# A fused decoder layer on one core: a new timetable by slots, six slots of attention output, and sums of v taken from wider products

## The reference

```python
scores = einsum('bsnh,btnh->bnst', k, q) / sqrt(32)
scores = triu(scores) + -10000.0 * tril(ones, k=-1)
attn = softmax(scores, axis=2)
out = einsum('bnkq,bknh->bqnh', attn, v)          # then @ Wo + bo
x = layernorm(x + attention(x))
x = layernorm(x + wkv(w, u, k=x, v=ctx))          # a scan over t, 512 channels
h = silu(x @ Wg.T) * (x @ Wu.T)                   # Wg, Wu, Wd: (int - 128) * scale
x = layernorm(x + h @ Wd.T)
```

## Time and profile before

| | us |
|---|---|
| median of 3 runs | 807.76 (806.75 to 809.14) |
| profiled execution | 813.54 |
| its span | 811.7 |
| PE busy in the span | 738.0 (91%) |
| DVE, ACT, POOL busy | 514.1, 437.6, 271.4 |
| mean granted clock of PE | 0.966 |

### The profile page before, as it was taken

The page is one execution under the profiler, slowest core; times in us unless marked ns, Lnnn a source line. Parts: engine busy times, 40 slices in busy tenths (PEclk is TensorE's granted clock), DMA queues, the critical chain, the costliest instruction groups (busy, mean ns, idle before and its releaser), DMA issues.

```text
span 811.7 us, 11923 instructions
## 1 busy us (share of the span) xinstructions
PE 738.0 (91%) x4256; PEld 402.2 (50%) x4256; DVE 514.1 (63%) x1132; ACT 437.6 (54%) x1035; POOL 271.4 (33%) x285
## 2 busy tenths in 40 slices
PE   6899799988989969979788999999998999999996
PEld 2465456654566536645454544445443444444443
DVE  3565575887998867678865377985758462342124
ACT  5678776877667767656587456405452234113310
POOL 2001310326571154233211454445655233113310
PEclk9899899997999979989999999999999999999999
DMA  8435384341324233253200810000000000010001
GB/s 265 118 91 169 96 205 130 92 117 43 89 78 139 91 83 92 74 131 57 78 1 1 156 52 0 14 27 14 0 1 20 34 0 1 14 40 0 1 14 39
DMA packets 45387, 54.17 MB, mean 67 GB/s; under 512 B 4752, under 2 KB 34704, under 8 KB 45328
## 3 DMA queue, kind: packets, MB, share of 16 engines
q1 hardware_dynamic: 42064, 47.11, 19.4%
q0 software_dynamic: 3264, 6.29, 4.5%
HBM read 47.10 MB, written 12.58 MB: 74 GB/s over the span
## 4 chain that ended last, share of the span: by engine, by line
PE 52%; DVE 17%; ACT 9%; POOL 8%; issue 8%; DMA 4%; SPq 1%; POOLq 0%; DVEq 0%; ACTq 0%
PE psb L779 16%; PE psb L665 5%; PE psb L714 5%; PE psb L792 4%; PE psb L790 4%; DVE ek L1114 4%; PE psb L759 4%; PE psb L681 3%; PE psb L727 3%; PE psb L703 2%; POOL ct L1267 2%; POOL ek L1271 2%; ACT ee L872 2%; DVE x L1089 2%; DVE ee L1018 2%
## 5 line engine op out<-in xcount | busy, mean ns | idle before, releaser
L1018 DVE CUSTOM_DVE_ANT_0 ee<-psb,mask,clip 128x512 f32<-128x512 f32 (+3 forms) x256 | 131.9, 534 | 62.9 <-PE psb L703 62.4
L872 ACT ACTIVATE ee<-ee,nm 128x512 f32<-128x512 f32 (+3 forms) x256 | 142.6, 558 | 33.8 <-DVE nm L1018 33.5
L1301 POOL TENSOR_TENSOR hl<-hf,hh 128x512 f16<-128x512 f32 x64 | 78.0, 1218 | 162.1 <-ACT hh L949 162.1
L883 ACT ACTIVATE ee<-psb 128x512 f32<-128x512 f32 (+1 forms) x192 | 100.0, 521 | 55.9 <-PE psb L714 37.5
L714 PE MATMUL psb<-ident,ee 128*128 128x128 f32 x640 | 108.8, 287 | 23.4 <-ACT ee L883 23.3
L949 ACT ACTIVATE hh<-hf 128x512 bf16<-128x512 f32 x64 | 40.3, 629 | 136.0 <-DVE hf L1141 131.2
L1141 DVE SCALAR_TENSOR_TENSOR hf<-th,c,psb 128x512 f32<-128x512 f32 x60 | 44.2, 737 | 105.2 <-PE psb L779 75.4
L714 PEld LDWEIGHTS psb<-ident,ee 128*128 128x128 f32 x640 | 77.2, 147 | 50.9 <-ACT ee L883 33.3
L792 PE MATMUL psb<-wd,hl 128*128 128x512 f16 x256 | 97.7, 382 | 3.7 <-POOL hl L1301 3.7
L790 PE MATMUL psb<-wd,hh 128*128 128x512 f16 x256 | 97.5, 381 | 0.9 <-ACT hh L949 0.9
L779 PE MATMUL psb<-x2h,wg 128*128 128x512 f16 x256 | 97.0, 379 | 1.3 <-ACT x2h L927 1.3
(11 more groups left out here) (111 smaller groups left out, 1205.9 us busy)
## 6 DMA issues: line engine op xcount, KB each, us to landing
qs<-parts SPq DMA_DIRECT2D x64, 128.0 KB, 2.9
ks<-parts SPq DMA_DIRECT2D x64, 128.0 KB, 3.2
parts<-qhl SPq DMA_DIRECT2D x16, 256.0 KB, 2.2
parts<-khl SPq DMA_DIRECT2D x16, 256.0 KB, 2.3
x<-in_x SPq DMA_DIRECT2D x4, 1024.0 KB, 7.4
ct<-in_ctxT SPq DMA_DIRECT2D x4, 1024.0 KB, 6.8
out<-x SPq DMA_DIRECT2D x16, 256.0 KB, 2.0
xt<-in_xT SPq DMA_DIRECT2D x14, 256.0 KB, 3.9
```

Source lines behind the costliest of these rows:

```text
L872: e.activation(dst, dst, ACT.Exp, bias=NM[:, n % 4, col:col + 1], scale=-1.0, accum_out=DEN[:, n % 4, col:col + 1]).then_inc(sem("exp"), 1)
L883: e.activation(ET[h][:, base:base + width], PSB[:, bank["turn", H, item], 0:width], ACT.Copy).then_inc(sem("et"), 1)
L1018: e.tensor_tensor_reduce(E[H % 3][:, EOFF[i]:EOFF[i] + w], PSB[:, bank["score", H, i], 0:w], MASK[:, S - w:S], -SC, CLIP[:, i:i + 1], ALU. ...
L1301: e.tensor_tensor(HS[it][1][:], ring(b, it)[1][:], HS[it][0][:], ALU.subtract).then_inc(sem("hl"), 1)
```

## The change

1. `timetable()` takes the slot of each piece from tables by group or batch, in place of a few offsets for all: `QK_AT`, `V_AT`, `WO_AT` (where the parts of a product are spread), `FIN_AT` (for each group the slots, counted from the start of the next, of `pv`, of `sv` with the first `spread`, and of the second), `XLOAD` and `XSPLIT`, `WKV_AT`, `YT_AT`, `X2_AT`, the loads and the subtraction of the zero point. `WAIT` sets how many slots behind its product each further step stands. `stack` becomes a piece of its own with a slot.
2. `oh` and `ol` have six slots in place of four (`OHS`); group n waits for `wo` of the batch of group n - 6. `HOLD` goes.
3. `later` and its copy go. The triangle of `sv` now takes in the diagonal, so that the first column of each block is the block's sum; `t1` reads its operand shifted by one column, and two additions of one column each (`SUF`) make the sums over later blocks, once a group. The last position's weight is set to zero by a product with `some` on POOL.
4. `EX` and `RX` become one tile `WIDE`; the second widening (`widen`) waits until PE has transposed the first.
5. `x2h` and `x2l` stand one and two slots behind `x2t`. The zero point of `wd` is taken off at 16 slots, not two a slot.

```diff
-WKV_AT = {(0, 0): (6, 6), (0, 1): (6, 15), (0, 2): (7, 4), (0, 3): (7, 10), (1, 0): (10, 6), (1, 1): (11, 4),
-QOFF, V0, V1, U0, U1, U2, W0, W1, W2, W3 = 11, 2, 11, 3, 4, 13, 3, 12, 0, 6
-XLOAD, XSPLIT = (14, 15, 18, 19), (1, 2, 5, 6)
-NSLOT, SP2, HOLD = (3, 1, 1, 1), 3, 11
+OHS = 6
+QK_AT = {2: (6, 19), 3: (22, 31), 4: (36, 46), 5: (62, 67), 6: (71, 79), 7: (88, 94), 8: (109, 112), 9: (123, 128),
+FIN_AT = {0: (2, 1, 11), 1: (2, 2, 13), 2: (2, 1, 11), 3: (1, 4, 9), 4: (2, 0, 10), 5: (2, 2, 11), 6: (0, 0, 9),
+XLOAD = {1: (11, 22, 28, 31), 2: (73, 86, 90, 95), 3: (156, 160, 162, 164)}
+XSPLIT = {1: (33, 33, 35, 36), 2: (96, 98, 100, 107), 3: (162, 168, 171, 173)}
+WKV_AT = {(0, 0): 109, (0, 1): 118, (0, 2): 124, (0, 3): 134, (1, 0): 176, (1, 1): 186, (1, 2): 212, (1, 3): 226}
...
-        def later(b):
-            bk = bank["later", b]
...
-            for g in range(T):
-                for j in range(1, T):
-                    mm = e.matmul(PSB[:, bk, 4 * g:4 * g + 4], VV[:, b % 2, j, g * P:(g + 1) * P],
-                                  LT[:, P + 4 * j:P + 4 * j + 4], start=(j == 1), stop=(j == T - 1))
...
             act.wait_ge(*by("t3", n))
-            if b:
-                act.wait_ge(*by("wo", b - 1, T - 1))
-            e.activation(oh[:, g, :], EB[:], ACT.Identity, bias=BV[:, g:g + 1]).then_inc(sem("oh"), 1)
+            if n >= OHS:
+                act.wait_ge(*by("wo", (n - OHS) // T, T - 1))
+            e.activation(oh[:, n % OHS, :], EB[:], ACT.Identity, bias=BV[:, g:g + 1]).then_inc(sem("oh"), 1)
...
+            sums = PSB[:, bank["sv", n], :]
+            e.tensor_scalar(SUF[:, 1:2], sums[:, 2 * P:2 * P + 1], sums[:, 3 * P:3 * P + 1], None, ALU.add).then_inc(sem("suf"), 1)
             dve.wait_ge(*by("eb", n))
-            dve.wait_ge(*by("suf", b))
-            for i in range(T):
...
+            e.tensor_tensor(EB[:, 3 * P - 1:S - 1], sums[:, 3 * P:S], EB[:, 3 * P - 1:S - 1], ALU.mult)
+            dve.wait_ge(sem("suf"), 2 * n + 1)
+            e.tensor_tensor(SUF[:, 0:1], sums[:, P:P + 1], SUF[:, 1:2], ALU.add).then_inc(sem("suf"), 1)
+            for i, rest in ((2, sums[:, 3 * P:3 * P + 1]), (1, SUF[:, 1:2]), (0, SUF[:, 0:1])):
...
+            e.tensor_tensor(EM[:, n % 4, :], EM[:, n % 4, :], SOME[:], ALU.mult).then_inc(sem("some"), 1)
...
+        def widen(n):
+            pool.wait_ge(*by("expand", n))
+            pool.wait_ge(sem("spread0"), n + 1)
```

More of the change, by code:

```diff
@@ L256, in yt @@
         add("yt", b, t)
-        late(3, residual)
+        late(WAIT["r2"], residual)
     def x2t(b, c):
@@ new lines, in spread_over, with piece, split_wo @@
+    def spread_over(units, first, end):
+        for k, u in enumerate(units):
+            at(first + k * (end - first) // len(units), u)
+    def piece(slot, *what):
+        at(slot, lambda: add(*what))
+    def split_wo():
+        add("split_wo")
+        add("load_ct", 0)
+    spread_over(vs0[3:], 0, 9)
+    for n, span in QK_AT.items():
+        spread_over(qk_units(n), *span)
+        begun = 16 * (n - 2) + 12
+        at(max(begun, span[1] + WAIT["low"]), lambda n=n: (tt.flush(("put", n, "k")), add("stack", n)))
@@ L368, in timetable @@
+    for which, slot in WKV_AT.items():
+        at(slot, lambda which=which: wkv(*which))
     slot_turn = ((1, 2), None, (0, 0), (0, 1))
```

275 lines of the change are left out of this document (121 added, 154 removed).

## The result

The changed kernel takes 765.74 us (median of 4 runs, 762.17 to 766.27) against 808.45 us of the kernel before (4 runs in the same series). The ratio is 0.946, interval 0.9422 to 0.9499; on the 807.76 us of the time shown ahead that is 764.1, a gain of 44. One caution: in a second series, of five rounds, it gave 769.07 us (6 runs) and a ratio of 0.9524, interval 0.9499 to 0.9549, a gain of 38. So the gain is 38 to 44 us. The forecast was 31, with a range from 765 to 799: the first series lies just outside it, the second inside. The direction was right, the size about a quarter too small.

A forecast was written before the change was run, and what follows sets the result against it. PE's work plus its waits and half clock, mostly in attention, was taken as the bound. Terms -12.0 + 1 - 19 - 5 + 2 + 1 + 3.5 - 3 = -31.5 took 813.5 to 782, stated as 777 against the 807.8 median; range 765 to 799.

The forecast's parts named there:

- The narrow products: Four blocks of `later` on PE's path: 10.3 us go, plus 1.7 of half clock; 12.0 taken, bounds 7 to 12.
- The triangle: Product `sv` on PE: the triangle keeps its 128 columns, so it costs PE nothing more.
- The splits: Three stalls where PE waits for ACT and ACT for late loads of x: gain 19 of 25.8 us, bounds 10 to 25.
- The projection: At 345 to 365 us PE idles, mostly for `ol` of the last group: gain 5 of 7.9 us.
- DVE's stretch in slots 112 to 143: From 200 to 240 us DVE sets the pace; group 7 loses work to group 8: 3 back, 4 charged, net +1.
- the 15 below which the prediction called itself wrong: Sign of failure: PE's busy time in attention falls by less than 15 us.
- the first stall: Batch 1's split of x: ACT still waits about 2.7 us, PE meets it directly; 4.7 of 7.4 us left.
- It goes better: Rival, 763 us: all 25.8 of stalls and 12 of products go, DVE's stretches lose half their idle time; chance 0.07.
- The rival of the clock: Slots 48 to 95 get thinner PE work and half clock there uses up the gain; 812 us; chance 0.06, slower.
- In slots 216 to 223 ... +3.5: Four `x2l` on DVE atop norm and reciprocals, with nine parts of `qk` and `wo` on PE: 3.5 us more.
- In the feed-forward ... -3: PE idles 2.0 and 2.8 us where transposes wait for a norm; `x2t` moves further behind it: 3 us less.
- What is put behind the early loads on SP is `put` and `stack`, but they are wanted eight or more slots later: Loads on SP's queue: those put behind the early x loads are wanted eight or more slots later, about 1.6 us each.

The follow-up runs named there:

- three sets of delays: Changed kernel with old delays put back one set each: norm 781.3 us; wkv steps 779.8; second residual with halves of the feed-forward's input 775.3.
- the three parts and the slots: Kernel before plus new sums of v, earlier loads and splits of x, feed-forward's places, and five output slots without hold; all together 795.4 us, ratio 0.9842.
- the kernels in the old order: Kernel before with parts of the change, alone or together, attention's own order kept; 806.3 us (output slots alone) to 790.2 (three parts, slots, some delays).

## Why the prediction was short

**What held.** The time is PE's work plus its waits and half clock, and most of what went was in attention. The narrow products cost PE what the row said: 10.3 us forecast, with 1.7 of half clock; 11.7 and 11.4 us measured at their places, the 1.7 behind the second block included. As a term of the time they gave 5.2 us alone in the old order, since half clock elsewhere took the rest, and cost 5 to 11 when put back. The Trainium skill, "TensorE: Matmul & The Clock Gate", section "Wait — 56ns, not 53.3ns?", gives a floor of some 25 ns between matmuls. An estimate by it would have made the 96 records 2.4 us; the trace has 11.1 us for them, far above the floor. The triangle cost PE nothing that the traces show. The splits: forecast 19, measured 12 to 17 by taking them back. The projection: slots 200 to 207, where `ol` was waited for, went from 17.3 us to 11.1, forecast 5. DVE's stretch in slots 112 to 143 went from 56.3 to 57.2, forecast +1. PE's busy time in attention fell by 22.7, above the 15 below which the prediction called itself wrong.

**What came out right by luck.** In batch 1 the prediction had ACT wait some 2.7 us for the third piece, and left 4.7 us of the first stall. Waits and clock in slots 32 to 39 are indeed 4.7 us, but ACT waits for `xt` there for 0.24 only, at the fourth piece:

```profile
75.65 0.63 ACT L828 ACTIVATE xh<-xt 128x512 f16<-128x512 f32 x1 [0.24 <-DMA xt<-in_xT]
```

What PE waits for is the split itself (1.2 us), copies and `weigh`. The time is that of the rival *It goes better* (763), but not by its way: not all of the stalls went, and what came on top came from the feed-forward and the delays. The rival of the clock went the other way: thin slots 48 to 95 run at full clock but for the new stall.

**What failed.**

1. *"In slots 216 to 223 ... +3.5".* The step counted what stands on DVE and PE in these slots and took each extra as exposed. Measured 16.0 to 15.7. The crowd was real: these slots have 2.4 us more of products, as counted. But PE's idle time in them fell from 4.9 to 2.2. It overlooked that the norm, too, moves with its new delay out of the way of the low halves; with the old delay the slots take 19.9, almost what the step had said. The edit that dissolves the crowd was in the change, in `WAIT`, and I had counted slots of products only.

2. *"In the feed-forward ... -3".* Two idle places were summed. The size of the term was 9.3. In the old order the places give about half of it and the delays the other half, and PE has no wait left at all between its first and second group of `y`. The middle stretch, before:

```profile
508.70:602.30 93.60, 88.89 (x435) 42.98 (x433) 68.83 (x95) 37.85 (x54) 48.95 (x43) 1.00 0.03 12
```

and after:

```profile
469.70:557.30 87.60, 87.60 (x430) 42.68 (x429) 64.30 (x97) 38.43 (x56) 50.97 (x44) 1.00 0.03 13
```

3. *The sum takes terms one by one.* The delays have no term at all in it, and they carry 26 to 32 us in the new order (`WAIT` back: 795.3). Nor do terms add in the new order: taken back one by one, splits, products and three sets of delays cost 43 to 70, more than the whole gain. In the old order the three parts and the slots give 17.1 us by their ratios and 12.8 together, a difference within the noise of five ratios. The reading that in the old order a removed stall exposes the next one, and that in the new one a single misplaced step makes a stall with half clock behind it, fits the slots shown above; as a rule it is argued, not shown.

4. *A stall that nobody forecast.* The change put two weight loads of GpSimd's ahead of the keys of group 5; this costs 6 us in the medians of one series and 3.4 in the other. "What is put behind the early loads on SP is `put` and `stack`, but they are wanted eight or more slots later" looked at SP's order only, not at what else is in flight.

That the lengths of the first stretches came out nearly right is in part luck. Products moved between them (2.2 us more in slots 0 to 47, 10 fewer in 48 to 143), which the forecast did not count. And over all 192 slots waits and clock fell by 12.8 us, with the new stall of 7 us in them; the others fell by 20, where the forecast had about 17.

What stays open: how much of the 20 to 26 us that none of the kernels in the old order shows belongs to the order of the products alone and how much to the wkv delays, the five other delays of `WAIT`, the sixth slot and `WIDE`. In the old order none of these was tried; in the new one the wkv delays are worth 10 to 15, and the others were not put back.

## What to carry to other kernels

When a change moves many places, read the delays as closely as the places: ask of every short step on a shared in-order engine what it waits for when it is reached, and what stands behind it. Sum a forecast for such a change by stretches, with the products of each stretch counted apart from its waits, and widen it on both sides: of the terms here, the splits and the narrow products gave less than forecast, the feed-forward three times as much, and the delays had no term. Where runs have their clock on record, compare span times clock as well as time: it tells a part that gives nothing from one whose gain the clock takes back. Before trusting an unchanged queue, look at every other queue that is active in the same ten microseconds.

## What the hardware showed that I had not expected

Transfers of SyncE took longer here not only to land but to be issued while loads of GpSimd's ran. Issues of the changed kernel between 118 and 134 us (KB each, median us to landing):

```profile
qs<-parts SPq DMA_DIRECT2D x4, 128.0 KB, 2.8
ks<-parts SPq DMA_DIRECT2D x4, 128.0 KB, 8.6
```

and between 119 and 131 us with the weight loads away:

```profile
ks<-parts SPq DMA_DIRECT2D x4, 128.0 KB, 3.3
```

Two loads of 512 KB by GpSimd take the landing from 3.3 to 8.6 us, four issues from 1.85 to 2.70 and one issue of x from 0.50 to 2.48; the DMA engines are 99% busy in slots 72 to 79, against 81% without the two loads. The repeats of both kernels show the same (9.0 and 3.3 us to landing). The second surprise is the clock in thin work. Slots 48 to 71 of the changed kernel (columns of the stretches):

```profile
91.20:121.80 30.60, 29.35 (x229) 18.64 (x227) 19.01 (x65) 25.52 (x71) 8.68 (x12) 1.00 0.22 61
```

Of the 229 records 72 are transposes of 128 columns (11.2 of the 29.35 busy us), PE is idle for 1.25 us of it in small gaps, and the granted clock is 1.00 throughout. In the same kernel it is 0.78 in slots 72 to 79, with 5.3 us idle.
